# A four-level perceiver on one core: tokens chosen by rows in SBUF with two bits a round, expert sums of two tiles in turns, and rotation ahead of scores

## Time and profile before

| | |
|---|---|
| median of 3 runs | 4343.03 us (4342.07 to 4351.01) |
| the profiled execution | 4323.21 us, span 4321.4 us |
| busy in the span | PE 77%, PEld 54%, DVE 60%, ACT 50%, POOL 40% |
| mean granted PE clock | 0.873 |

### The profile page before, as it was taken

One profiled execution on the slowest core, in us unless ns is written; L12 is line 12 of the kernel. 1 busy time (PEld: TensorE's weight loads), 2 busy tenths in 40 slices (PEclk: granted clock), 3 DMA queues, 4 the chain that ended last, 5 costly groups with the idle time before them and its releaser, 6 DMA issues. The chain is left out here.

```text
span 4321.4 us, 88069 instructions
## 1 busy us (share of the span) xinstructions
PE 3334.7 (77%) x26791; PEld 2351.5 (54%) x26791; DVE 2578.9 (60%) x6100; ACT 2164.0 (50%) x6493; POOL 1715.7 (40%) x1532
## 2 busy tenths in 40 slices
PE   6979475879999667658699998688873366967966
PEld 4758223657777566435477776233323243844644
DVE  6856564547777545243577777598884412445862
ACT  5544314877777534322566665454541013646964
POOL 4610100005655567015255554588870160104830
PEclk9989577999999889869799999799995586977978
DMA  3300001222222100012011110343322033920000
GB/s 94 89 8 0 6 0 37 82 64 66 67 67 66 35 7 1 5 59 61 23 30 29 29 30 20 128 138 137 138 99 82 16 49 100 240 51 6 2 4 22
DMA packets 139158, 236.15 MB, mean 55 GB/s; under 512 B 27940, under 2 KB 99910, under 8 KB 138159
## 3 DMA queue, kind: packets, MB, share of 16 engines
q1 hardware_dynamic: 130824, 224.23, 17.5%
q0 software_dynamic: 8128, 9.45, 1.2%
HBM read 202.66 MB, written 14.11 MB: 50 GB/s over the span
## 5 line engine op out<-in xcount | busy, mean ns | idle before, releaser
L2367 POOL TENSOR_TENSOR l2x_att_prob<-l2x_att_prob,l2x_att_rs 128x1028 f32<-128x1028 f32 x128 | 243.2, 1900 | 276.5 <-DVE l2x_att_rs L2552 276.5
L3063 PE MATMUL l2a_pY<-l2a_hc,ident 128*128 128x512 f32 x512 | 275.3, 677 | 89.5 <-POOL l2a_hc L2980 55.3
L2511 ACT ACTIVATE l2x_att_prob<-l2x_att_pS,l2x_att_nmx 128x257 f32<-128x257 f32 x512 | 236.3, 474 | 209.8 <-DVE l2x_att_nmx L2547 209.8
L2367 POOL TENSOR_TENSOR l1x_att_prob<-l1x_att_prob,l1x_att_rs 128x1028 f32<-128x1028 f32 x128 | 243.2, 1900 | 207.4 <-DVE l1x_att_rs L2552 207.4
L2511 ACT ACTIVATE l1x_att_prob<-l1x_att_pS,l1x_att_nmx 128x257 f32<-128x257 f32 x512 | 236.3, 475 | 148.1 <-DVE l1x_att_nmx L2547 147.9
L2950 POOL TENSOR_TENSOR l2a_dbu<-l2a_dx,l2a_BC 128x1024 f32<-128x1024 f32 x128 | 298.4, 2352 | 21.0 <-PE l2a_pY L3063 10.7
L3080 ACT ACTIVATE l2a_pA<-l2a_dl,l2a_A 128x512 f32<-128x512 f32 x256 | 174.5, 689 | 187.8 <-DVE l2a_pH L3186 112.5
L2563 DVE COPY l1x_att_probT<-l1x_att_pT 86x512 f32<-86x512 f32 x256 | 175.3, 685 | 115.9 <-PE l1x_att_pT L2453 108.2
L3063 PEld LDWEIGHTS l2a_pY<-l2a_hc,ident 128*128 128x128 f32 x512 | 103.8, 212 | 252.6 <-issue 120.3
L2563 DVE COPY l2x_att_probT<-l2x_att_pT 86x512 f32<-86x512 f32 x256 | 175.7, 686 | 108.3 <-PE l2x_att_pT L2453 108.3
L3186 DVE TENSOR_TENSOR_SCAN l2a_pH<-l2a_pA,l2a_dbu 128x512 f32<-128x512 f32 x192 | 224.8, 1216 | 23.2 <-POOL l2a_dbu L2950 12.2
(11 more groups left out here) (726 smaller groups left out, 9329.3 us busy)
## 6 DMA issues: line engine op xcount, KB each, us to landing
l2a_BC<-l2a_rows SPq DMA_DIRECT2D x128, 512.0 KB, 3.8
l3x_att_ctn<-ctx_n SPq DMA_DIRECT2D x32, 576.0 KB, 11.5
l0x_att_kvs<-ctx_t SPq DMA_DIRECT2D x32, 514.0 KB, 3.5
l1x_k_xin<-ctx_t SPq DMA_DIRECT2D x32, 514.0 KB, 3.5
l1x_att_ctx<-ctx_t SPq DMA_DIRECT2D x128, 128.5 KB, 2.1
l1x_att_kT<-l1x_KA SPq DMA_DIRECT2D x128, 128.5 KB, 2.2
l2x_att_ctx<-ctx_t SPq DMA_DIRECT2D x128, 128.5 KB, 2.1
l3x_att_ctx<-ctx_t SPq DMA_DIRECT2D x32, 514.0 KB, 9.4
```

Source lines behind the costliest of these rows:

```text
L2367: pool.tensor_tensor(p, p, bc(rs[:, b, :], 2, KEYS), ALU.mult).then_inc(scaled, 1)
L2511: last = act.activation(prob[:, b, j, 0:KEYS], pS[:, j, 0:KEYS], ACT.Exp, bias=nmx[:, b, j:j + 1], accum_out=sums[:, b, j:j + 1])
L3063: last = pe.matmul(pY[c][:, :], env.ident[:, :], hc[:, u % 3, c, :], start=False, stop=n == NS - 1)
```

## The change

1. `linear_experts` is written out tile by tile, without hardware loops and without ACT's copies; PE reads `XNT` and `WT` as they are. There are three sets of two product banks, freed half by half. DVE works on two tiles in turns: bias of one, bias of the other, then for each expert one tile and then the other. Each sum waits for the one two places ahead of it. After the two biases, and after experts 3 and 7, DVE waits for everything before it and frees banks.
2. `route` writes W with the experts outside the tiles, and no longer makes `WT`. `choose_tokens` turns W by two 128x128 transposes into `pc`, whose row now holds one expert's values of two neighbouring tiles; nothing goes through DRAM, and `pc` and `pos` stay in SBUF for `list_tokens`, which turns them by two transposes each.
3. The threshold is found with two bits a round: 15 rounds with three comparisons each, which count as they compare (`accum_out`), one matmul of four columns, one instruction that tests and keeps, and a maximum over four.
4. In self attention DVE's `rotate(n+2)` stands ahead of `scores(n+1)`.

The core of the diff:

```diff
-            @block.scalar
-            def _(act):
-                with act.Fori(0, TILES // 2) as i:
...
             @block.tensor
             def _(pe):
                 pe.wait_ge(loaded, 32)
+                for n in range(TILES):
+                    r = slice(n * P, (n + 1) * P)
+                    if n >= 2:
+                        pe.wait_ge(b_used, n - 1)
+                    pe.matmul(pb[n % 2][:, 0:D], WT[:, r], be[:, :]).then_inc(b_made, 1)
+                    for h in range(2):
+                        if n >= 3:
+                            pe.wait_ge(y_used[h], n - 2)
+                        pe.matmul(py[n % 3][h][:, :], env.XNT[:, r], we[:, h * 512:(h + 1) * 512]
+                                  ).then_inc(y_made[h], 1)
...
+                def expert(n, e):
+                    dve.wait_ge(added, n // 2 * 2 * STEPS + 2 * (e + 1) + n % 2 - 1)
+                    h = e // 4
+                    if e % 4 == 0:
+                        dve.wait_ge(y_made[h], n + 1)
...
+                for n in range(0, TILES, 2):
+                    for t in (n, n + 1):
+                        bias(t)
+                    dve.wait_ge(added, n * STEPS + 2)
+                    dve.sem_inc(b_used, 2)
+                    for e in range(EXPERTS):
+                        for t in (n, n + 1):
+                            expert(t, e)
+                        if e % 4 == 3:
+                            dve.wait_ge(added, n * STEPS + 2 * (e + 2))
+                            dve.sem_inc(y_used[e // 4], 2)
...
-                sp.dma_start(scratch, WT[:, :]).then_inc(moved, 16)
-                sp.wait_ge(moved, 16)
-                sp.dma_start(pc[:, :], rows(scratch)).then_inc(landed, 16)
                 sp.dma_start(same[:, :], env.a.c_same_expert).then_inc(landed, 16)
...
-                sp.dma_start(rows(scratch3), pos[:, :]).then_inc(moved, 16)
-                sp.wait_ge(moved, 32)
-                sp.dma_start(PT[:, :], scratch3).then_inc(written, 16)
-                sp.wait_ge(written, 48)
...
+                for j in range(2):
+                    done = pe.transpose(pw[:, j * P:(j + 1) * P],
+                                        W[:, :, j:TILES:2].rearrange("p e c -> p (e c)"), env.ident[:, :])
+                done.then_inc(turned, 1)
...
+                with dve.Fori(0, ROUNDS) as k:
+                    dve.wait_ge(step, 3 * k + 1)
+                    dve.tensor_tensor(cand[:, :].bitcast(I32), thr[:, 0:1].bitcast(I32).to_broadcast([P, 4]),
+                                      bits[:, bass.ds(4 * k, 4)], ALU.bitwise_or).then_inc(step, 1)
+                    dve.wait_ge(step, 3 * k + 2)
+                    for j in range(1, 4):
+                        count = dve.tensor_scalar(gts[:, j - 1], pc[:, :], cand[:, j:j + 1], None, ALU.is_ge, ALU.add,
+                                                  accum_out=cnts[:, j:j + 1])
+                    count.then_inc(counted, 1)
                     dve.wait_ge(summed, made(k))
+                    dve.scalar_tensor_tensor(out=kept[:, :], in0=ps[:, 0:4], scalar=float(CAP), in1=cand[:, :],
+                                             op0=ALU.is_ge, op1=ALU.mult).then_inc(step, 1)
+                    dve.wait_ge(step, 3 * k + 3)
+                    dve.tensor_reduce(thr[:, :], kept[:, :], AX.X, ALU.max).then_inc(step, 1)
...
                     if inside(n):
                         factors(n)
+                    if inside(n + 2) and not cross:
+                        rotate(n + 2)
                     if inside(n + 1):
                         scores(n + 1)
-                    if inside(n + 2) and not cross:
-                        rotate(n + 2)
```

More of the change, by code:

```diff
@@ L414, in _ @@
                 sp.dma_start(be[:, :], b_d).then_inc(loaded, 16)
-            @block.scalar
-            def _(act):
-                with act.Fori(0, TILES // 2) as i:
-                    for s in range(2):
-                        n = 2 * i + s
-                        act.wait_ge(y_ready[s], before(i))
-                        act.activation(xs[:, s, :], env.XNT[:, bass.ds(n * P, P)], ACT.Copy)
-                        act.activation(ws[:, s, :], WT[:, bass.ds(n * P, P)], ACT.Copy).then_inc(staged[s], 1)
             @block.tensor
@@ L427, in _ @@
                 pe.wait_ge(loaded, 32)
-                with pe.Fori(0, TILES // 2) as i:
-                    for s in range(2):
-                        pe.wait_ge(staged[s], made(i))
-                        pe.wait_ge(y_used[s], before(i))
-                        for h in range(2):
-                            pe.matmul(py[s][:, h * 512:(h + 1) * 512], xs[:, s, :], we[:, h * 512:(h + 1) * 512])
-                        pe.matmul(pb[s][:, 0:D], ws[:, s, :], be[:, :]).then_inc(y_ready[s], 1)
+                for n in range(TILES):
[8 more added lines that the diff above has]
+                                  ).then_inc(y_made[h], 1)
@@ L436, in _, with bias @@
             @block.vector
             def _(dve):
[L438 to L450 removed]
+                def bias(n):
+                    dve.wait_ge(b_made, n + 1)
+                    x = env.X[:, n, :]
+                    dve.tensor_tensor(x, x, pb[n % 2][:, 0:D], ALU.add).then_inc(added, 1)
@@ L624, in choose_tokens @@
         same, lower = st.sb("same", [P, P]), st.sb("lower", [P, P])
-        bits = st.sb("bits", [P, BITS], I32)
-        thr, cand, keep, cnt, need = (st.sb(n, [P, 1]) for n in ("thr", "cand", "keep", "cnt", "need"))
-        ps = st.ps("ps", [P, 512])
-        moved, landed, written = st.sem("moved"), st.sem("landed"), st.sem("written")
+        bits = st.sb("bits", [P, 4 * ROUNDS], I32)
+        cand, kept, cnts = (st.sb(n, [P, 4]) for n in ("cand", "kept", "cnts"))
+        thr, cnt, need = (st.sb(n, [P, 1]) for n in ("thr", "cnt", "need"))
@@ L629, in choose_tokens @@
+        ps, pw = st.ps("ps", [P, 512]), st.ps("pw", [P, 512])
+        landed, turned, copied, zeroed = (st.sem(n) for n in ("landed", "turned", "copied", "zeroed"))
         step, counted, summed = st.loop_sem("step"), st.loop_sem("counted"), st.loop_sem("summed")
-        ready, placed, zeroed = st.sem("ready"), st.sem("placed"), st.sem("zeroed")
         with nc.Block() as block:
@@ L1066, in _ @@
             def _(pe):
-                for n in range(TILES):
-                    last = pe.transpose(pp[:, n * EXPERTS:(n + 1) * EXPERTS], PT[:, n * P:(n + 1) * P],
-                                        env.ident[0:EXPERTS, 0:EXPERTS])
-                last.then_inc(turned, 1)
-                for n in range(TILES):
-                    last = pe.transpose(pw[:, n * EXPERTS:(n + 1) * EXPERTS], WT[:, n * P:(n + 1) * P],
-                                        env.ident[0:EXPERTS, 0:EXPERTS])
-                last.then_inc(turned, 1)
+                for out, rows in ((pp, pos), (pw, pc)):
+                    for j in range(2):
+                        last = pe.transpose(out[:, j * P:(j + 1) * P], rows[:, j * P:(j + 1) * P], env.ident[:, :])
+                    last.then_inc(turned, 1)
                 for h in range(2):
@@ L3665, in layouts @@
     o["L3_ffn_up_b"] = v["L3_ffn_up_b"]
-    o["bits"] = np.tile((1 << np.arange(29, -1, -1)).astype(np.int32), (P, 1))
+    o["bits"] = np.tile(np.outer(1 << np.arange(28, -1, -2), np.arange(4)).reshape(-1).astype(np.int32), (P, 1))
     o["L0_attn_Wq"] = v["L0_attn_Wq"]
```

152 lines of the change are left out of this document (49 added, 103 removed).

## The result

The kernel before took 4344.07 us on the chip that ran both (4 runs, 4342.07 to 4351.01), the changed one 4176.75 us (4 runs, 4167.39 to 4188.06): the ratio is 0.9623 (95% interval 0.9605 to 0.9641). That is 167 us less; the forecast was 155 less, 4188 us in a range of 4168 to 4220.

The account below looks back on a forecast made before the run. No engine bounds the whole: stages meet at barriers, each as long as its slowest chain. Gains 61 + 19 + 29 + 46 = 155 us; 4343.0 - 155 = 4188 us, range 4168 to 4220.

Parts of the forecast that it names:

- the reading of 0.496: Level-0 experts before: sums start 0.496 us apart though 0.351 long, so DVE waits about 0.145 for each predecessor.
- the four scalings: Normalisation's four independent DVE scalings, 0.257 us apart though 0.340 long; their 0.083 overlap priced the new sums at 0.27.
- The upper bound: Level-0 experts: each sum starts only when its predecessor has ended, 0.38 us apart, gaining 37 us instead of 61.
- The rival by the Trainium skill: Level-0 experts: the next operation waits for an empty pipe, so sums don't overlap, 0.38 us apart; total 4212; chance 0.12.
- The rival of the half clock: Level-0 experts: PE stays at clock 0.50, a pair takes 9.1 us, gain 5 instead of 61; total 4244; chance 0.08.
- the seam: Between `pos` and the listing's first issue: 8.8 us before, 1.8 taken to stay, gaining 7.0 (bounds 6.0 and 7.4).
- The price of counting: Choice of tokens: x, the extra time of counting while comparing, taken as 0.1 us for each of three comparisons a round.
- a second pass: Choice of tokens: counting while comparing costs a whole further pass, x = 0.42 us, adding 14 us; total 4202; chance 0.07.
- 31 rounds x 1.46: Self attention: the round falls from 6.56 to 5.1 us, 45 us over 31 rounds; with the first rotation, 46.
- stopped neither at 5.6: Self attention: the round stops at 5.6 us, the chain returning to POOL having only 0.45 slack; total 4203; chance 0.09.
- for want of the projection: Self attention: the rotation waits at DVE's queue head for PE's projection and blocks the scores; slower overall; chance 0.02.
- The 20 us by which the profiled execution lay under the median: Profiled execution of the kernel before, 4323.2 us, against the runs' median; the difference was taken to stay, no reason known.

Follow-up runs that it names:

- Experiment 1: Changed kernel with level-0 expert sums made tile by tile again, each waiting for the one before it, still written out: stage 171.7 us, 28.1 longer; ratio 0.9677.
- experiment 3: Changed kernel with the choice of tokens back at 30 one-bit rounds, still without DRAM: stage 304.1 us, 27.2 longer; ratio 0.9671 to the kernel before.
- experiment 7: Changed kernel with the three comparisons not counting and one separate reduction summing their flags: stage 284.5 us, 7.6 longer; ratio 0.9656 to the kernel before.
- Experiment 2: Changed kernel with DVE's rotation put back behind the scores in self attention: stage 269.7 us, 53.5 longer; ratio 0.9728 to the kernel before.
- experiment 8: Changed kernel with one of POOL's two additions per tile in level 1 self attention given to DVE: stage 219.7 us, 3.5 longer; ratio 0.9616.
- experiment 4: Changed kernel without DVE's full stops in the level-0 experts, PE waiting on the count of sums: stage 131.9 us, 11.7 shorter; ratio 0.9545.
- experiment 9: Changed kernel without DVE's full stops in the level-0 experts and with the choice's rounds written out: 4140.93 us, ratio 0.9572; changed kernel beside it 4164.54 us.

## Why the prediction was right, point by point

**Part 1, -61 predicted, -65 measured.** From PE's start (510.03) to the last sum (601.5) are 91.5 us; forecast 96. Sums 0.26 apart (0.27), pair 5.38 (5.6): a full stop leaves 0.21 or 0.22 and not 0.25, as the text had allowed (5.4). The start-up cost 5.4 (6.5). PE was granted the full clock, 1.00 from 520 to 590 us and busy 64.3 of 70. The step that was wrong in its reason is the reading of 0.496: it was put down to waiting for the predecessor. Experiment 1 has the same wait at 0.386; three quarters of the 0.145 were the loop. The size came out right because the new sums were priced from the four scalings, which stand outside a hardware loop, so that the loop's cost left the sum without having been seen; of the 61 us credited to the turns they brought 28. That is luck in the reason, if not in the number. The upper bound, sums 0.38 apart and -37 in all, is what experiment 1 measured to the half us. The text called 0.27 the floor though its own row gave 0.257; 0.26 was measured.

The rival by the Trainium skill (VectorE: DVE Perf Modes, "The DRAIN you can't avoid") fell: sums with three operands, each behind a wait whose count was already there, began 0.08 us before their predecessors ended. What the section adds, that some operations start earlier, is what happened here. The rival of the half clock fell too.

**Part 2, -19 predicted, -20.2 measured** up to the listing's first step, -18.4 as what is left of the whole stage (experiment 3). 11.3 us ahead of the first round (53.5 to 42.2 from the stage's start), forecast 11.55; the strided write of W took 0.59 against 0.42. Behind `pos` the seam is 1.06, the same kind that I had read as 1.4 and raised to 1.8: 7.7 gained where 7.0 were forecast. The listing's first step gained 1.05, forecast 0.8. The three together are 20.1.

**Part 3, -29 predicted, -27.2 measured.** The price of counting was taken as 0.1 and is 0.13; in the first round the three comparisons and the readout take 1.29 us for the 1.19 forecast, and from the test to the next candidate are 0.75 for 0.67: the loop's return idles 0.39 in place of 0.25 to 0.28, and the new threshold is 0.06 shorter. The unknown was bracketed between nothing and a second pass, and lay near the end that was chosen; experiment 7 is what rules the second pass out.

**Part 4, -46 predicted, -52.7 measured.** The steady round is 5.03, forecast 5.1. The mis-sized term is 31 rounds x 1.46: it took every round for a steady one. The row maximum's starts are (1618.0 - 1465.0) / 31 = 4.94 apart and were (1734.6 - 1529.1) / 31 = 6.63 before: 31 x 1.69 = 52.5. But the first four rounds took 27.3 us before, at a granted clock of 0.87, and take 17.2 now, at 1.00: 10.1 saved where four steady ones save 6.1. Experiment 2 has the slow first rounds and the lower clock back with the order. The rounds stopped neither at 5.6 nor for want of the projection: DVE idled before the first two rotations (4.1 us together), and never in the steady rounds.

**The sum.** 4188 forecast; stages that gave 163.6 in place of 155, and a median 167 lower. Of the 8.6 us between the first two, 7 are part 4 (4 its first four rounds, the rest a shorter steady round and its last rounds) and 4 part 1 (a pair of 5.38 for 5.6, and the start), less 2 in parts 2 and 3. Up to the listing's first step those two gave 47.4 of the 48 forecast; the other 2 us are the spread behind it. The remaining 4 us between 163.6 and 167 lie within the spread of the untouched stages. The 20 us by which the profiled execution lay under the median are as large as that spread. To take them to stay was a guess that held for the first set, where the median was 4344; beside the later sets it was 4333 and 4325.

## What to carry to other kernels

Write out a short-bodied loop before giving its instructions turns: here the writing out was worth 37 us and the turns on top of it 28. Before moving an addition of two SBUF operands from GpSimd to VectorE, look at what GpSimd runs at that moment: here it waited for GpSimd in 30 of 32 tiles. Where an engine idles ahead of a late input while something short and ready is queued behind it, swap them, and price the pipeline's first rounds apart from the steady one. When a change touches separate stages, compare stage by stage over two profiles, since one untouched stage moved by 24 us, as much as a part's gain.

## What the runs showed of the hardware that had not been expected

**A DVE addition of two SBUF operands beside POOL's work** took 0.962 us in the median and 0.285 at best, and ended 0.14 to 0.16 us behind the POOL instruction that was running when it began (experiment 8). DVE instructions there that read one operand from PSUM, as the rotation at 0.41, kept their length. The Trainium skill (Trainium Architecture — The Big Picture, "What this means for kernel authors") says that VectorE and GpSimd share a pair of SBUF ports under an exclusive lock. The trace agrees: the addition ended late by just what was left of POOL's instruction, and at full speed where POOL was idle. No run moved the addition's operands to PSUM to try it the other way round.

**The clock of one short burst of PE differs between executions.** The router's products at the head of level 2's feed-forward ran at 0.50 in the changed kernel and at 0.73 over a like stretch of experiment 4, whose edit is far away:

```profile
3167.00:3188.00 21.00, 20.22 (x96) 20.13 (x96) 2.18 (x10) 8.30 (x17) 0.00 (x0) 0.50 0.31 86
```

```profile
3145.00:3160.00 15.00, 14.24 (x96) 14.10 (x96) 2.54 (x12) 8.32 (x18) 0.00 (x0) 0.73 0.45 125
```

The same 96 products, in code that is the same, take 14.2 us in place of 20.2, and from the stage's start to the first round are 35.7 us in place of 42.2. It was so in experiments 4, 8 and 9, and at 42 in the other eight profiles of this form. PE had been idle before the burst for 22.5 to 22.8 us in those three and for 23.1 to 23.2 in all the others, the kernel before included, where the burst also ran at 0.50. The two go together in all thirteen profiles; which of them follows from the other, or both from something else, no run shows.

**The level 1 experts' stage**, which the change doesn't touch, was 187 to 195 us in eight profiles and 207 to 215 in five: the first one of the changed kernel and those of experiments 1 to 4, which ran in one set. The kernel before was timed beside them at medians of 4344.07 and 4350.05, and beside the later sets, whose profiles have the short form, at 4332.85 and 4325.47. So the length seems to belong to the time or the chip of a set and to strike both kernels, since the ratio hardly moved (0.9623 and 0.963); but neither profile of the kernel before has it, so this is not shown. Stretches of the two profiles of the changed kernel (columns as in the earlier trace rows), the first, then the second:

```profile
1868.00:1884.00 16.00, 13.31 (x73) 8.91 (x72) 5.97 (x16) 4.35 (x16) 9.90 (x11) 1.00 0.15 46
...
1900.00:1916.00 16.00, 14.39 (x67) 9.82 (x67) 4.87 (x14) 3.66 (x13) 8.78 (x9) 0.79 0.14 42
```

```profile
1860.00:1876.00 16.00, 15.61 (x87) 10.63 (x86) 7.07 (x19) 5.83 (x21) 12.29 (x13) 1.00 0.19 55
```

In 16 us PE gets through 67 to 73 products in place of 87. In the first the list of waits has ACT 16.5 us behind "remote" in five places and DVE 8.4 in five; in the second there is none. The granted clock fell to between 0.79 and 0.89 in some stretches, with PE less busy. What "remote" stands for the profile doesn't say, so what held the engines stays open.
